# First attention: the max units of a step moved together, behind its first three scores

## The reference, cut to what matters

```python
q = jnp.concatenate([q_sem, q_geo], axis=-1)      # 16 heads, 32 numbers each, half of them rotated
k = jnp.concatenate([k_sem, k_geo], axis=-1)
scores = jnp.einsum('bhqd,bhkd->bhqk', q, k).astype(jnp.float32) * scale
scores = jnp.where(causal, scores, jnp.finfo(jnp.float32).min)
attn = jax.nn.softmax(scores, axis=-1).astype(v.dtype)
out = jnp.einsum('bhqk,bhkd->bhqd', attn, v)
```

## Time and profile before

| | |
|---|---|
| time, median of 3 runs | 2674.24 us (2671.98 to 2675.84) |
| the profiled execution | 2672.64 us, of it the span 2670.9 us |
| TensorE busy, of the span | 2313.3 us (87%), mean granted clock 0.92 |
| VectorE, ScalarE, GpSimd busy | 46%, 28%, 22% |
| the first attention's exponentials | from 180.6 to 786.3 us of the span |

### The profile page before, as it was taken

The page is one execution under the profiler, slowest core; times in us unless marked ns, Lnnn a source line. Parts: engine busy times, 40 slices in busy tenths (PEclk is TensorE's granted clock), DMA queues, the critical chain, the costliest instruction groups (busy, mean ns, idle before and its releaser), DMA issues. The chain is left out here.

```text
span 2670.9 us, 28189 instructions
## 1 busy us (share of the span) xinstructions
PE 2313.3 (87%) x10204; PEld 1559.1 (58%) x10204; DVE 1227.4 (46%) x2284; ACT 743.9 (28%) x1344; POOL 596.2 (22%) x398
## 2 busy tenths in 40 slices
PE   7977999999977797888747668799999799999997
PEld 5854555554525443333325546588888578787875
DVE  6754767766605421111144444222222655555556
ACT  3322555555553211000122222112112321111222
POOL 4342546555650130000012222000000302020200
PEclk9976999999998898898868779899999899999998
DMA  5474444432105231111142332511110300000001
GB/s 185 158 177 103 108 115 105 112 70 64 25 17 211 94 114 45 59 55 55 55 144 70 116 110 89 212 40 47 47 40 28 131 1 32 16 32 16 32 16 48
DMA packets 112368, 213.06 MB, mean 80 GB/s; under 512 B 11184, under 2 KB 29104, under 8 KB 110960
## 3 DMA queue, kind: packets, MB, share of 16 engines
q1 hardware_dynamic: 103152, 181.43, 22.1%
q0 software_dynamic: 8240, 27.01, 3.0%
q10 hardware_dynamic: 864, 3.15, 0.3%
HBM read 136.44 MB, written 75.10 MB: 79 GB/s over the span
## 5 line engine op out<-in xcount | busy, mean ns | idle before, releaser
L614 ACT ACTIVATE a_probs<-a_stb 128x512 f32<-128x512 f32 (+3 forms) x640 | 309.1, 535 | 282.6 <-PE a_stb L726 166.8
L585 POOL TENSOR_TENSOR a_probs<-a_probs 128x1024 f32<-128x1024 f32 (+3 forms) x160 | 281.7, 1773 | 288.7 <-PE a_avb L738 273.5
L640 DVE TENSOR_REDUCE a_mparts<-a_sbank 128x1 f32<-128x512 f32 x384 | 239.7, 683 | 101.3 <-PE a_sbank L700 101.1
L56 PE MATMUL m_gu<-hi,m_wh 128*128 128x512 f32 x512 | 204.3, 399 | 15.8 <-DVE m_h L2056 14.4
L1988 POOL CAST m_wh<-m_wst 128x1024 fp32r<-128x1024 f32 x24 | 27.9, 1162 | 786.3 <-DMA m_wst<-in_w_mlp 424.0
L57 PE MATMUL m_gu<-lo,m_wh 128*128 128x512 f32 x512 | 202.7, 396 | 0.0
L58 PE MATMUL m_gu<-hi,m_wl 128*128 128x512 f32 x512 | 202.5, 396 | 0.0
L700 PE MATMUL a_sbank<-hi,q 96*128 96x512 f32 (+3 forms) x320 | 135.4, 453 | 24.5 <-PEq L152 12.8
L1245 DVE TENSOR_TENSOR e_h<-e_h,e_ab 128x256 f32<-128x256 f32 x39 | 16.4, 421 | 304.7 <-ACT e_h L1169 304.7
L738 PE MATMUL a_avb<-a_probs,V 128*32 128x512 f32 (+3 forms) x1280 | 154.8, 556 | 0.7 <-ACT a_probs L614 0.7
L645 DVE CUSTOM_DVE_ANT_0 a_junk<-a_sbank,hidden 128x128 bf16<-128x128 f32 (+3 forms) x256 | 113.5, 487 | 82.3 <-PE a_sbank L700 80.6
(11 more groups left out here) (248 smaller groups left out, 4879.1 us busy)
## 6 DMA issues: line engine op xcount, KB each, us to landing
qk<-v_hl SPq DMA_DIRECT2D x32, 512.0 KB, 2.9
hi<-qk SPq DMA_DIRECT2D x60, 256.0 KB, 4.8
lo<-qk SPq DMA_DIRECT2D x60, 256.0 KB, 5.8
q<-qk SPq DMA_DIRECT2D x48, 256.0 KB, 5.6
m_wst<-in_w_mlp SPq DMA_DIRECT2D x24, 512.0 KB, 3.3
xs<-a_zeros POOLq DMA_DIRECT2D x39, 256.0 KB, 2.5
xt<-xs SPq DMA_DIRECT2D x39, 256.0 KB, 2.8
ys<-e_rows_b SPq DMA_DIRECT2D x39, 256.0 KB, 2.0
```

What stands on the lines that cost most here:

```text
L56: nc.tensor.matmul(out, wh, xh, start=start, stop=False, skip_group_check=True)
L585: nc.gpsimd.tensor_tensor(probs[:, i % PSLOTS, hs, w0:], probs[:, i % PSLOTS, hs, w0:], probs[:, (i + 1) % PSLOTS, hs, w0:], ALU.add)\
L614: nc.scalar.activation(probs[:, i % PSLOTS, h, w0:], stb[:, k % 3, w0:], ACT.Exp, scale=SCALE0)\
L640: nc.vector.reduce_max(to, sbank[:, b, :], AX).then_inc(s["unit_max"], 1)
```

## The change

The loop that writes `order` puts the first three scores of a step side by side, then everything of its four gaps, then the value product of the step before and its denominator, then the fourth score:

```diff
-        for h in range(4):
-            if h == 3 and i > 0:
-                order.append(("av", i - 1))
-                if i >= 3 and i % 2:
-                    order.append(("den", i - 3))
-            order.append(("scores", i, h))
-            order += in_gap[k]
-            k += 1
+        order += [("scores", i, h) for h in range(3)]
+        for gap in in_gap[k:k + 4]:
+            order += gap
+        k += 4
+        if i > 0:
+            order.append(("av", i - 1))
+            if i >= 3 and i % 2:
+                order.append(("den", i - 3))
+        order.append(("scores", i, 3))
```

## The result

After: 2795.94 us median (2790.88 to 2806.22, 4 runs). Before, on the same chip: 2673.11 us. The ratio is 1.0466 [1.0431, 1.0501]: 4.7% slower, 123 us. I had forecast 2778 (2748 to 2830), so the direction and the range held and the sum was 18 us short. The profiled execution of after took 2793.05 us, its span 2791.3, 120.4 more than before's; what comes before item 0's first value product (187.96 us before, 188.87 after, +0.9) and behind the first attention (1882.4 us against 1884.5) hardly moved.

A forecast was written before the change was run, and what follows sets the result against it. TensorE, in its given order, was taken to bound the first attention. Items 0 to 3 +3, 4 to 7 +20, 8 to 11 +43, 12 to 14 +39, 15 0: +105 us on 2672.6 gives 2778 (2748 to 2830).

The forecast's parts named there:

- The score's wait: First attention: with no units between scores, score 2 waits for the exponential three scores back; 0.5 us a step.
- The bank's wait: Bursts of units share three `sbank` banks: the fourth unit starts 1.15 us after the first instead of 0.70.
- What goes away: Item starts: VectorE's transposes and reciprocal no longer hold up units; saving already in the tail's steps; turns cost 3 us.
- The collision: Item starts in before: units stand behind VectorE's transposes and denominator reciprocal, a matmul idle 0.50 us; would go away.
- DMA and queues: Loads keep their order, GpSimd's work comes later; two more scores ahead of each wait for queries, under 1 us each.
- The term that was mis-sized: Items 4 to 7: before's one fall to 1.2 GHz, some 4 us, half of which comes back.
- Rival A: First attention: two idle pieces a step make TensorE's granted clock fall; +175 us, 2850; chance 0.12.
- the main case: First attention: the score and bank waits add in series, +105 us to 2778, own range 2750 to 2805; chance 0.77.
- A's own sign: Profile after: a granted clock under 0.9 in the first attention's middle would show the falling clock.
- Rival B: First attention: only one of the two waits counts; +50 us, 2725; chance 0.05.
- Rival C: Item starts and turns: the collision and the waits for maxima go, so faster, 2652, -20 at most; chance 0.03.
- TensorE's busy share in the middle: Profile after: TensorE's busy share in the first attention's middle falls to near 80 to 85%, from 97.6%.

The follow-up runs named there:

- e3: After, with each maximum taken over 128 of its keys only and the exponential's scale divided by 64; 2715.93 us, ratio 1.0161.
- e7: After, with the third score behind the gathered units (order of e1) and maxima over 128 keys only (as e3); 2673.54 us, ratio 1.0001.
- e1: After, with the units still together but behind the second score, ahead of the third; 2745.29 us, ratio 1.0265.
- e9: Before, with VectorE's three denominator instructions at item starts (items 4 to 13) put one behind each of the next three units; 2668.16 us, ratio 0.9987.
- e11: After, with the units on the diagonal computed over all 512 keys, so their matmuls are no longer narrow; 2798.22 us, ratio 1.0464.
- e12: Before, with the units on the diagonal computed over all 512 keys; 2686.03 us, ratio 1.0044.
- e4: After, with the first unit of a step's burst issued once more, unused, ahead of the third score from item 4 on; 2800.25 us, ratio 1.0486.
- e8: Before with the change of e9, and the turn (transpose of the maxima) planned two gaps later; 2661.63 us, ratio 0.9961.
- e10: After, reordered: two scores, three gaps of units together, third score, value product, fourth score, fourth gap; 2700.61 us, ratio 1.0109.
- e5: Before, with each maximum taken over 128 of its keys only and the exponential's scale divided by 64; 2642.98 us, ratio 0.9881.

## Why the prediction was right, and where its sum fell short

1. *The score's wait.* Forecast 0.5 us, measured 0.49 (3.73 in e3 against 3.24 in e7). In all, taking it out of after saves 51 us (e1), less than 0.5 in each step with units, and with 20 us less at half clock: the two waits overlap in irregular steps, where an item's start is 5.06 us in after and 5.03 in e1.
2. *The bank's wait.* Forecast 0.45 and 0.11 of restart, measured 0.57 (e1 against before). Together the regular step got 1.07 longer (3.07 to 4.14), against 1.06 forecast.
3. *What goes away.* The collision is real in before (e9), and it went as forecast: the step at item 12's start, with four units and a denominator, was 0.88 us above the regular one (4.80 against 3.92) and is 0.07 above it in after (5.06 against 4.99). It got longer all the same, because the regular step did.
4. *DMA and queues.* The wait for queries was 12.3 us in two, less than before's; later stages only shifted. Everything up to the end of item 3 took 6.0 us more (0.9 and 5.1), for which the sum had 3, within its -3 to +8.
5. *The term that was mis-sized* is the clock, for whose falls the sum had 2 us in items 4 to 7 and nothing elsewhere. Rival A and the main case were not exclusive, as I had set them up. A's own sign, a clock under 0.9 in the middle, did not show (0.96, 0.93 and 0.98), and the regular steps kept 1.0 in spite of their two idles. But between them the clock fell nine times instead of once: eight times among the diagonal steps, and once, at 841.4 us, in a step of full scores, seven of whose eight units were 128 or 256 keys wide. At 1.1 to 1.6 us for each 3.4, the 47.8 us at half clock are 15 to 22 us. Over items 4 to 14 the sum missed by 14.4 us (116.4 against 102). Most of it sits where the falls are: items 8 to 11 missed by 12.6 us with 30.7 us at half clock (10 to 14 us by that price), and in e11, with 10.2, they take 224.3, of which up to 2.9 are the wider matmuls (e12); 221 is within 4 of the 217. That items 12 to 14 came out at 207.9 against 208 is in part luck: they hold 6.8 us at half clock, 2 to 3 us, which the sum did not have, so its other terms are that much too high there. The rest of the 18 us is the first items' 3, less 2.1 that the later stages took less, and 2.4 between the profiled span's 120.4 and the medians' 122.8, well within the spread of runs.

The Trainium skill, "TensorE: Matmul & The Clock Gate", section on psum-queue depth-cycling, says that short idles between groups of matmuls which cycle through PSUM banks make the clock swing. The trace agrees in part: regular steps with two waits each held 1.00 (the tail's too), stretches of narrow matmuls with waits between them did not. That the narrow ones matter is supported by e11, where widening some removed most falls, but not settled: e4 moved falls without touching them, e11's fall at 534.3 us came behind wide ones only, and no run kept both the order and the clock. What starts a fall stays open.

Rival B fell: e1 and e3 each take one wait away, and each gains. Rival C's gain exists (e9 gives 5 us, e8 12) but doesn't need this change and is a tenth of the new waits' price. Of the forecast signs one was wrong: TensorE's busy share in the middle is 90% (522 of 582 us), not 80 to 85. Matmuls that waited are recorded longer (0.50 for 0.39) and those at half clock twice as long, so the share hides both losses; step lengths don't.

## What to carry to other kernels

Order on an engine that is the bound is a matter of distances: with three buffers, count the time from one use to the third next, and compare it with the time until the consumer lets go. Spread work of two consumers, so that each is another's cover; one unit put back among the scores was worth 84 of 123 us, some of it by the clock. Where several small instructions of an off-path engine stand in a row ahead of work that frees buffers, put the buffer's work between them.

## What I had not expected of the hardware

- In these traces a bank had to be free some 0.1 us *before* its matmul's turn, because the wait sits on the weight load: e10 lost 0.10 us with a bank only 0.02 late, e7 0.17 with one 0.07 late.
- The clock fell for short stretches (3.4 to 10.2 us) inside the dense stage, and one of 3.4 us cost only 1.1 to 1.6 us by the estimates from e4 and e11.
- Where before's matmuls waited 7.5 us for the maxima (items 4 to 14), it gained 22 us when these got shorter (466.1 to 443.8 us in e5). The waits on weight loads, 19.1 us, were nearer to the truth, and a fall of the clock of 10.2 us went with them.
